# Context attention's opening: angles in pieces, rows copied sooner, low parts on VectorE

## What is computed

```
q  = rope(rms_norm(draft @ Wq.T, q_norm_w), draft_positions)
kv = concat([context, draft])
k  = rope(rms_norm(kv @ Wk.T, k_norm_w), all_positions)
v  = kv @ Wv.T
out = softmax(q k.T / sqrt(128)) v @ Wo.T
```

## Time and profile before

| | |
|---|---|
| median of 3 runs | 2946.42 us (2940.98 to 2946.8) |
| the profiled execution | 2945.43 us |
| its span | 2943.6 us |
| TensorE busy | 2687.9 us, 91% of the span |
| VectorE busy | 1920.8 us, 65% |
| ScalarE busy | 1595.7 us, 54% |
| GpSimd busy | 1319.5 us, 45% |

### The profile page before, as it was taken

The page is one execution under the profiler, slowest core; times in us unless marked ns, Lnnn a source line. Parts: engine busy times, 40 slices in busy tenths (PEclk is TensorE's granted clock), DMA queues, the critical chain, the costliest instruction groups (busy, mean ns, idle before and its releaser), DMA issues. The chain is left out here.

```text
span 2943.6 us, 48843 instructions
## 1 busy us (share of the span) xinstructions
PE 2687.9 (91%) x16828; PEld 1531.7 (52%) x16828; DVE 1920.8 (65%) x3585; ACT 1595.7 (54%) x3661; POOL 1319.5 (45%) x1344
## 2 busy tenths in 40 slices
PE   6789886799999999859977999999889999999998
PEld 4667672355555555424434666665654444444443
DVE  5778896788787787677656788886473233332335
ACT  7999983565656565464327777776442222222121
POOL 3889896876676766223324111111032222222121
PEclk8999998999999999989987999999989999999999
DMA  5111114322221211150011000000032111111211
GB/s 164 41 54 48 42 37 132 73 44 40 43 39 39 45 37 36 22 172 36 1 35 59 16 20 18 15 16 23 8 96 68 49 52 66 64 68 33 68 33 68
DMA packets 153698, 148.79 MB, mean 51 GB/s; under 512 B 108689, under 2 KB 113169, under 8 KB 151858
## 3 DMA queue, kind: packets, MB, share of 16 engines
q1 hardware_dynamic: 153522, 146.49, 17.8%
HBM read 112.57 MB, written 4.52 MB: 40 GB/s over the span
## 5 line engine op out<-in xcount | busy, mean ns | idle before, releaser
L2092 POOL TENSOR_TENSOR s_state<-s_state,s_ct 128x512 f32<-128x512 f32 x256 | 327.1, 1310 | 79.8 <-DVE s_state L2267 77.3
L797 POOL TENSOR_TENSOR m_aTl<-m_prod,m_aTh 128x512 bf16<-128x512 f32 x88 | 101.8, 1157 | 559.6 <-ACT m_aTh L871 559.6
L2267 DVE TENSOR_TENSOR_SCAN s_state<-s_decay,s_psd 128x512 f32<-128x512 f32 x256 | 301.7, 1208 | 66.5 <-PE s_psd L2412 32.4
L1056 DVE TENSOR_TENSOR m_prod<-m_bank,m_gated 128x512 f32<-128x512 f32 x88 | 60.9, 692 | 406.6 <-ACT m_gated L869 406.6
L869 ACT ACTIVATE m_gated<-m_bank 128x512 f32<-128x512 f32 x88 | 52.5, 597 | 403.0 <-PE m_bank L1187 220.5
L1170 PE MATMUL m_bank<-m_xTh,m_wh 128*128 128x512 bf16 x704 | 267.5, 380 | 2.0 <-DVE m_prod L1056 1.2
L1171 PE MATMUL m_bank<-m_xTl,m_wh 128*128 128x512 bf16 x704 | 267.3, 380 | 0.0
L2412 PE MATMUL s_psd<-ident,s_v 128*128 128x128 f32 x1024 | 163.4, 284 | 42.9 <-DVE s_state L2267 21.5
L2168 ACT ACTIVATE s_decay<-s_dt,s_nega 128x508 f32<-128x508 f32 x256 | 181.7, 711 | 18.8 <-DVE s_state L2267 18.6
L2181 ACT ACTIVATE s_v<-s_uT,s_bT 128x512 f32<-128x512 f32 x256 | 182.2, 713 | 0.2
L2412 PEld LDWEIGHTS s_psd<-ident,s_v 128*128 128x128 f32 x1024 | 120.7, 145 | 90.3 <-ACT s_v L2181 48.6
(11 more groups left out here) (511 smaller groups left out, 8084.1 us busy)
## 6 DMA issues: line engine op xcount, KB each, us to landing
s_ct<-ssm_bc SPq DMA_DIRECT2D x64, 256.0 KB, 3.2
m_scale<-moe_scale SPq DMA_DIRECT2D x64, 256.0 KB, 3.2
m_stage<-in_moe_w_dram SPq DMA_DIRECT2D x16, 768.0 KB, 4.9
m_stage<-in_moe_w_dram SPq DMA_DIRECT2D x8, 1024.0 KB, 8.4
X<-in_x_dram SPq DMA_DIRECT2D x4, 1024.0 KB, 12.7
a_cf<-in_ctxT_dram SPq DMA_DIRECT2D x16, 256.0 KB, 2.9
a_wstage<-in_xa_wq_dram SPq DMA_DIRECT2D x8, 512.0 KB, 3.9
a_wstage<-in_xa_wo_dram SPq DMA_DIRECT2D x8, 512.0 KB, 4.0
```

The source lines that it names most:

```text
L2092: pool.tensor_tensor(h, h, ct[t % 4][:, s * P:(s + 1) * P].unsqueeze(1).broadcast_to([P, KB, P]), ALU.mult).then_inc(weighted, 1)
L2267: dve.tensor_tensor_scan(state[i % RING][:, :], decay[t % 2][:, s, :, :].rearrange("p m t -> p (m t)"), ps_d[i % 2][:, :], 0.0, ALU.mult, ...
```

## The change

The diff does four things.

- `angles(1)` was done behind the six chunks of the opening. It is split into `angle_products` (five instructions) behind chunk 1, the first two of three remainders (four instructions) behind chunk 2, and the third (two) behind chunk 3.
- `bound(1)` on VectorE moves from behind the eight chunks to behind chunk 4, and `sine_part(1)` on ScalarE from there to behind chunk 5.
- `x_copy(2)` moves from turn 0, where it stood behind `tables(1)`, to ahead of `tables(1)`.
- The low halves of the output weights in turn 0, `wl.vector(..., *wo_part(g))`, move from the end of each group on GpSimd to the end of each group on VectorE.

```diff
             def angles(n):
+                angle_products(n)
+                angle_remainders(n, range(3))
+
+            def angle_products(n):
                 if late(n, 1):
                     pool.wait_ge(sines.sem, sines.at(n - 1))
...
-                for i in range(3):
+
+            def angle_remainders(n, which):
+                for i in which:
                     pool.wait_ge(angle.sem, angle.at(n, 5 + 2 * i))
...
                         if g == 0:
-                            x_copy(s + 2)
+                            if start != 0:
+                                x_copy(s + 2)
                             angles(s + 2)
...
                     if not last:
                         front(s + 1, g, 1 - p)
-                    if start == 0:
-                        wl.vector(pool, wlow, *wo_part(g))
...
             for c in range(6):
                 front_chunk(0, c, 0)
                 turned_low(0, c)
-            angles(1)
+                if c == 1:
+                    angle_products(1)
+                if c == 2:
+                    angle_remainders(1, (0, 1))
+                if c == 3:
+                    angle_remainders(1, (2,))
+            x_copy(2)
             tables(1, 1)
...
                 if c < 4:
                     wl.scalar(act, 2 * c + 5, 2 * c + 6)
-            sine_part(1)
+                if c == 5:
+                    sine_part(1)
...
                     if not last:
                         chunk(s + 1, 2 * g + 1, 1 - p)
+                    if start == 0:
+                        wl.vector(dve, wlow, *wo_part(g))
...
                 if c < 4:
                     wl.vector(dve, wlow, 2 * c + 4, 2 * c + 6)
-            bound(1)
+                if c == 4:
+                    bound(1)
```

## The result

The changed kernel took 2953.25 us (median of 8 runs, 2950.21 to 2958.12); the kernel before, run beside it, 2944.84 us (8 runs, 2940.98 to 2947.91). The ratio is 1.0029, 95% interval 1.002 to 1.0037: slower by 0.3%, a small but clear loss, where a gain of 2 us was forecast, and outside the range. The profiled execution took 2955.39 us with a span of 2953.6, 10.0 us over the span before.

What follows compares the result with a forecast made beforehand. TensorE alone was taken to set the pace once context attention runs, so the start of its unbroken stretch decides; the opening's terms summed to about -1.9 us, from 2945.43 to 2943.5 us, range 2938.0 to 2948.5.

Steps and rivals of the forecast that it cites:

- Angles and first exponentials: Opening: angles in pieces leave first maxima at 520.6 against 520.46, no gain; first exponentials at 522.06 against 522.74, taken as -0.6 us.
- Rival 1: Opening: angles hide in 5 us of room on GpSimd, first maxima at 515.5 to 516; 2938.5 us, chance 0.13.
- Price of the low parts: First turn, VectorE: each moved low part takes 1.22 us, a pair 2.45 us, at four places ahead of the next maxima.
- Rival 2: First turn's group ends: low parts collide on VectorE, sum nought at 1.54 us each, 2950 us at the slowest; chance 0.14.
- the rule that the prediction took from the Trainium skill: VectorE instruction with two SBUF inputs contends with GpSimd's SBUF reads as an exclusive lock; moved low parts would still collide.
- Normalizing: First turn, VectorE: four instructions fall from 6.55 to about 2.05 us (-4.5) and from 5.20 to about 2.0 (-3.2).
- The third and the fourth pair: First turn, VectorE: third pair of low parts costs 0.5 us instead of 2.45, fourth pair the full 2.45.
- shift: VectorE's scalar shift at 574.51 falls from 1.83 us to 0.3, -1.5, bringing the sum to -1.95.
- With TensorE unbroken from then on: From the product at 577.60 on, TensorE alone sets the pace, so the opening's shift of about -1.9 us reaches the end.
- rival 3: At 577.6 something other than VectorE's low half releases TensorE, shift absorbed: -1 to +1, 2945.4 us; chance 0.13.

## Why the prediction was wrong, step by step

**Angles and first exponentials: right.** First maxima at 521.01 with a stage 1.2 us late, so -0.7 (I had 520.6, a gain of nothing); first exponentials at 522.61, -1.3 with the same correction where I had -0.6. The rows were copied at 521.06, and TensorE no longer waits for them. Rival 1 (5 us of room on GpSimd) did not come.

**Price of the low parts: slightly low.** Eight on VectorE took 1.21 to 2.28 us, mean 1.43; the four pairs 2.73, 3.41, 2.74 and 2.56 us where I had 2.45 each. Their sum is 1.6 us over mine. Rival 2 asked for 1.54 a piece on three pairs; the first three pairs came to 1.48 a piece. By itself this rival does not carry the loss. Where the two engines meet it is as the rule that the prediction took from the Trainium skill, page "SBUF — State Buffer", section "Who interferes with whom", would have it: 3.41 us for a pair beside GpSimd's chunk work, whose low half there took 2.13 us instead of 1.16. The normalizing of the earlier trace rows, which the prediction counted as agreeing, is not the case that this rule names: it reads one large tile and not two.

**Normalizing: right, and better.** The four took 1.14 us in groups 1 and 2, where I had 2.05 and 2.0, against 6.55 and 5.20.

**The third and the fourth pair, 0.5 and 2.45 us: the first step that failed.** Up to there the sum held: corrected for the stage's start, `bound(2)` ended 4.4 us sooner (557.87 against 561.12), where I had 3.4. From its end to the reciprocal I had 8.4 us of VectorE's own work and ScalarE's exponentials. It took 11.6 (557.87 to 569.48), since 1.94 us for `a_sq` and 1.16 us for `a_woh` came in: 3.7 us over the 7.91 of before, not 0.5. From that reciprocal to the next maxima VectorE waited another 0.35 us for the values' high half, 2.04 us for `a_vh` and 0.32 us for `a_woh`: 4.3 us for the fourth pair, not 2.45. So the sum at TensorE's wait for `a_pTl` is

- mine: -1.95
- `bound(2)` 1.0 sooner; third pair +3.2; fourth +1.9; shift 1.7 less, not 1.5: -0.2
- together +1.9; measured, 580.67 against 577.60 less 1.2, +1.9.

The other 1.4 us up to the loop's entry came in turn 1, where TensorE had 0.92 of its clock and was busy 20.17 of 22.40 us. I had added up VectorE's queue as if its inputs would come as early as before. But the pairs ahead of the maxima hold back `a_pTl`, TensorE idles 4.5 to 5.7 us for it and comes back at the lower clock, and its products for the chunk that VectorE does next are late. The run with the pair half a group later shows that the order is what costs: the same instructions, on the same engine, gave -5.6 instead of +2.6 once `a_pTl` was not behind them, and 6.8 us of such waits of VectorE's were gone. How much of the loss is the lower clock and how much the plain waiting was not separated.

**"With TensorE unbroken from then on": the second step that failed**, and the larger one, 5.6 us. I read the earlier trace rows as saying that nothing behind the opening could change, since no line of the loop was touched. What changed is where the loop lies in VectorE's stream, and that twelve memsets alone bring the loss into the kernel before, and forty take it out of the changed one, shows that this place is the cause.

What came of "nothing arrives", rival 3: nothing; the wait for `a_pTl` did decide.

## What to carry to other kernels

When work is moved to another engine, ask of each place not what it costs there but what stands right behind it and who is idle for that: with the same pairs the opening was 3.3 us longer when they stood ahead of the maxima and 5.6 us shorter when they stood behind `a_pTl`, where VectorE was waiting anyway for part of the time. An instruction that is added or removed ahead of a hardware loop moves the loop in its engine's stream; when a loop that was not touched grows by the same amount at every return, look in the DMA view for instruction packets in it, and try a few idle instructions ahead of it. Such padding holds for one build only: the next edit moves the loop again.

## What the runs showed of the hardware

VectorE's loop of two turns was accompanied by instruction fetches at every return at some places in its stream and at none at others. Shifted by 0, 8 or 52 instructions against the kernel before, it had no instruction packet from its second to its fifth round; shifted by 12 or 20, it had 5 packets of 8 KB a round, four around the return and one in the middle. That cost about 1.1 us a return, 5.1 to 5.9 us over five returns, in seven kernels. Shifted by 12, the first maxima of the round are the late ones; shifted by 20, VectorE stands still for 1.18 us between the first maxima's shift and `a_pTl`. The work at the head of the round does not hide it, since TensorE waits there for VectorE (0.66 us, 0.92 us). The Trainium skill, page "Runtime: NRT & Kernel Launch", section "Instruction fetch mechanics", says that most engines hold 32 KiB of instructions in blocks of 16 KiB, 256 instructions, and that a taken branch to a page outside the window forces a fetch before work goes on. The traces agree in kind: a fetch around the branch back, and in some places only. An estimate from that page: a body of some 270 instructions, as this loop has in VectorE's compiled stream, spans two blocks in most places and three in a stretch of about 15, which is compatible with the stretch found (from between 9 and 12 on, 20 still in it, ended by 52). That the blocks' bounds lie there no run shows, nor how five packets of 8 KB go with blocks of 16 KiB. That it is VectorE's place that matters is shown by the shifts; whether another engine's loop would do the same was not tried.

The second surprise is the later stage whose granted clock differed between executions of nearly equal kernels (0.62 and 0.70 over the same work), worth some 3 us: a difference of two single profiles can hold that much that has nothing to do with the change, so a loss is better read from matching instructions in the stage than from the spans.
